# A Mamba-2 step's tokens turned by a transposing DMA instead of by TensorE

## The reference

```python
proj = hidden_states @ in_proj_w.T
gate, hBC, dt = jnp.split(proj, [INTER, INTER + CONV_DIM], axis=-1)
hBC = silu(causal_conv4(hBC) + conv_b)          # channel by channel, along the tokens
hs, Bx, Cx = jnp.split(hBC, [INTER, INTER + G * N], axis=-1)
dt = softplus(dt + dt_bias)
X = hs * dt                                      # tokens of a head, times dt
Y_diag = (C B^T * exp(segsum(A dt))) @ X         # within a chunk
states = (B * decay_to_end) ^T @ X               # of a chunk
Y_off = C @ previous_states * exp(cumsum(A dt))  # between chunks
xg = (Y_diag + Y_off + D * hs) * silu(gate)
out = groupwise_rms_norm(xg) @ out_proj_w.T
```

## Time and profile before

| | |
|---|---|
| median of three runs | 1616.51 us |
| the profiled execution, whole | 1617.07 us |
| its span | 1615.3 us |
| TensorE busy | 1598.4 us (99%) |
| VectorE busy | 1390.4 us (86%) |
| ScalarE busy | 1266.0 us (78%) |
| GpSimd busy | 1168.7 us (72%) |
| DMA queue of the loads | 41.7% of 16 engines |
| granted TensorE clock | 1.0 |

### The profile page before, as it was taken

How to read it: one execution, slowest core, us unless ns; L and a number is a source line. 1 busy time by engine, 2 the same in 40 slices (tenths; PEclk the granted TensorE clock), 3 DMA queues, 4 the chain that set the end, 5 groups by cost and what they waited for, 6 DMA issues and landing times. The chain is left out here.

```text
span 1615.3 us, 29072 instructions
## 1 busy us (share of the span) xinstructions
PE 1598.4 (99%) x9668; PEld 1342.4 (83%) x9668; DVE 1390.4 (86%) x2356; ACT 1266.0 (78%) x2496; POOL 1168.7 (72%) x1496
## 2 busy tenths in 40 slices
PE   8999999999999999999999999999999999999998
PEld 7888888888888888888878888888888888888887
DVE  6988888888888888898889888888888988888887
ACT  3678888888888888878846888888888888888885
POOL 5548777778687776878774587777777768777685
PEclk9999999999999999999999999999999999999999
DMA  5244443444434445344314444444454444434431
GB/s 174 92 150 128 136 143 122 149 129 134 148 118 149 133 130 150 119 146 130 119 51 144 133 131 147 122 145 131 133 150 123 141 134 129 151 126 138 143 120 63
DMA packets 82372, 212.18 MB, mean 131 GB/s; under 512 B 11184, under 2 KB 27568, under 8 KB 81968
## 3 DMA queue, kind: packets, MB, share of 16 engines
q1 hardware_dynamic: 82224, 210.33, 41.7%
HBM read 207.14 MB, written 3.15 MB: 130 GB/s over the span
## 5 line engine op out<-in xcount | busy, mean ns | idle before, releaser
L653 POOL TENSOR_TENSOR xl<-xg,xh 128x256 fp32r<-128x256 f32 x254 | 290.7, 1166 | 319.4 <-ACT xh L482 318.8
L558 POOL TENSOR_TENSOR wl<-raw,wh 128x256 fp32r<-128x256 f32 x584 | 425.4, 758 | 76.6 <-ACT wh L325 76.6
L353 ACT ACTIVATE mt<-cs_row,cs_tok 128x128 f32<-128x128 f32 x1024 | 324.8, 391 | 0.0
L667 POOL TENSOR_TENSOR wol<-raw_o,woh 128x256 fp32r<-128x256 f32 x256 | 181.5, 729 | 30.5 <-ACT woh L472 30.5
L1223 DVE TENSOR_TENSOR mt<-mt,gt 128x1024 f32<-128x1024 f32 x128 | 200.7, 1568 | 0.0
L660 POOL TENSOR_TENSOR sqa<-sqa,sq 128x256 f32<-128x256 f32 x222 | 158.9, 735 | 0.8 <-ACT sq L499 0.8
L482 ACT ACTIVATE xh<-xg 128x512 fp32r<-128x512 f32 x128 | 81.0, 633 | 95.4 <-DVE xg L1203 95.4
L325 ACT ACTIVATE wh<-raw 128x1024 fp32r<-128x1024 f32 (+1 forms) x146 | 152.1, 1042 | 0.8 <-DMA raw<-in_w_dtag 0.8
L1000 DVE SCALAR_TENSOR_TENSOR cv<-bt,par_sb,cv 128x511 f32<-128x511 f32 (+2 forms) x192 | 142.9, 744 | 6.8 <-ACT cv L329 2.3
L1000 DVE SCALAR_TENSOR_TENSOR cv<-bh,par_sb,cv 128x511 f32<-128x511 f32 (+2 forms) x192 | 142.9, 744 | 4.5
L717 PE MATMUL bg<-xTh,wh 128*128 128x512 f32 x544 | 145.8, 390 | 0.0
(11 more groups left out here) (218 smaller groups left out, 3601.7 us busy)
## 6 DMA issues: line engine op xcount, KB each, us to landing
raw<-in_w_step SPq DMA_DIRECT2D x128, 512.0 KB, 3.5
cs_row<-cs_rows SPq DMA_DIRECT2D x128, 512.0 KB, 5.5
raw_o<-in_w_out SPq DMA_DIRECT2D x128, 256.0 KB, 4.1
ec_row<-ec_rows SPq DMA_DIRECT2D x256, 96.0 KB, 4.7
raw<-in_w_bc SPq DMA_DIRECT2D x16, 512.0 KB, 3.6
acc<-in_x SPq DMA_DIRECT2D x8, 256.0 KB, 5.3
cs_row<-in_w_ffn SPq DMA_DIRECT2D x2, 1024.0 KB, 6.6
out_dram<-acc SPq DMA_DIRECT2D x1, 1024.0 KB, 6.2
```

What stands on the lines that cost most here:

```text
L353: e = act.activation(mt[:, m % 2, h, chunk(j)], cs_row[:, m % 2, h, chunk(j)], ACT.Relu, bias=cs_tok[:, j, 2 * m + h:2 * m + h + 1], scale ...
L558: e = pool.tensor_tensor(wl[:, n % 2, cols], raw[:, n % 2, cols], wh[:, n % 2, cols].bitcast(F32), ALU.subtract)
L653: e = pool.tensor_tensor(xl[:, u, cols], xg[:, u, cols], xh[:, u, cols].bitcast(F32), ALU.subtract)
L667: e = pool.tensor_tensor(wol[:, 1 - u, cols], raw_o[:, 1 - u, cols], woh[:, 1 - u, cols].bitcast(F32), ALU.subtract)
```

## The change

The four transposes leave TensorE for all steps of a sequence but the last (126 of 128 steps, m from 0 to 62). In their place:

1. ScalarE copies h2, seen as 1024 numbers of 16 bits per partition, into the buffer `tg` as two planes: all low halves, then all high halves (a_half).
2. SyncE issues one transposing DMA from there into `turned`, 128 partitions by 8 blocks of 128 numbers of 16 bits (ld_turn). It stands ahead of the loads of its iteration.
3. GpSimd joins the halves again with two copies into xt, one for each plane (p_tok).
4. VectorE's `take_tokens` reads xt from SBUF instead of a PSUM bank, and stands behind the three taps instead of ahead of the mask product. Its second product works in place and waits for the first.

The gate's tanh writes `tg` too, so it now waits for the DMA's landing. The small tensors of the router use the memory of `turned` before the steps begin. The last step of each sequence keeps the transposes.

The diff (left out: how the router's small tensors are laid into `spare`):

```diff
--- before.py
+++ after.py
@@ -7,6 +7,7 @@
 
 F32 = mybir.dt.float32
 F32R = mybir.dt.float32r
+U16 = mybir.dt.uint16
 ALU = mybir.AluOpType
 ACT = mybir.ActivationFunctionType
 AXX = mybir.AxisListType.X
@@ -120,6 +121,9 @@
         pick = sb("pick", [P, SQ])
         some = sb("some", [P, L // SQ])
 
+        turned = sb("turned", [P, 2 * NJ, P], U16)
+        halves = tg[:, :].bitcast(U16)
+
         gflat = gt[:, :, :].rearrange("p g c -> p (g c)")
         xn = gflat[:, 0:NJ * HID].rearrange("p (j d) -> p j d", j=NJ)
         um = gflat[:, 6 * L:7 * L].rearrange("p (j c) -> p j c", j=NJ)
@@ -132,18 +136,15 @@
         mv = sb("mv", [P, NJ, 2])
         ve = sb("ve", [P, NJ])
         rstd = sb("rstd", [P, NJ])
+        spare = turned[:, :, :].rearrange("p a b -> p (a b)").bitcast(F32)
...
         dab, dm, de = mt[:, 0, 0], mt[:, 0, 1], mt[:, 1, 0]
         dz, dw, dh, dden = sg[:, 0], sg[:, 1], tg[:, :], mt[:, 1, 1]
@@ -166,6 +167,7 @@
         ld_ec = [sem(f"ld_ec{i}") for i in range(2)]
         st_cs, st_out = sem("st_cs"), sem("st_out")
         v_pick, v_some = sem("v_pick"), sem("v_some")
+        a_half, p_tok, ld_turn = sem("a_half"), sem("p_tok"), [sem(f"ld_turn{i}") for i in range(2)]
         a_dr, p_acc, t_fin, v_xl = sem("a_dr"), sem("p_acc"), sem("t_fin"), sem("v_xl")
 
         pv, pa, pp, pe_ = sem("pro_dve"), sem("pro_act"), sem("pro_pool"), sem("pro_pe")
@@ -198,6 +200,23 @@
 
         def has(m):
             return 0 <= m < STEPS
+
+        def by_dma(m):
+
+            return 0 <= m < STEPS - 1
+
+        def turn(b, m):
+            return b * (STEPS - 1) + m
+
+        def wait_turned(eng, b, m):
+
+            if m < 0:
+                b, m = b - 1, m + STEPS
+            if b >= 0:
+                if by_dma(m):
+                    eng.wait_ge(a_half, did(turn(b, m)))
+                else:
+                    eng.wait_ge(t_t, did(b))
 
         def bank_y(b, m):
 
@@ -295,6 +314,11 @@
                 sp.wait_ge(p_ffn, b + 1)
                 for m in range(-2, STEPS):
                     n = b * STEPS + m
+                    if by_dma(m - 1):
+                        q = turn(b, m - 1)
+                        sp.wait_ge(a_half, did(q))
+                        sp.wait_ge(p_tok, did(q - 1))
+                        sp.dma_start_transpose(turned[:, :, :], halves).then_inc(ld_turn[q % 2], 16)
                     if m + 2 < STEPS or b + 1 < NB:
                         load(step(b, m + 2))
                     if has(m):
@@ -316,7 +340,7 @@
 
         @block.scalar
         def _(act):
-            start(act, (a_dr, a_tap, a_th, a_tg, a_rl, a_ex, a_s1, a_xh, a_sq, a_wh, a_wn, a_woh, a_bt))
+            start(act, (a_half, a_dr, a_tap, a_th, a_tg, a_rl, a_ex, a_s1, a_xh, a_sq, a_wh, a_wn, a_woh, a_bt))
             act.wait_ge(ld_hp, 16)
             act.activation(nA[:, 0:1], hp[:, 1:2], ACT.Exp).then_inc(scaled, 1)
 
@@ -505,6 +529,8 @@
                             tanh_conv(n, u, mine)
                         act.wait_ge(t_g, did(n))
                         act.wait_ge(v_sg, did(n - 1))
+                        if by_dma(m - 1):
+                            act.wait_ge(ld_turn[turn(b, m - 1) % 2], landed(turn(b, m - 1)))
                         act.activation(tg[:, :], bg[:, :], ACT.Tanh, scale=0.5).then_inc(a_tg, 1)
                         if m >= 2:
                             tanh_conv(n, u, mine)
@@ -512,6 +538,12 @@
                         weights_and_state()
                     if m == STEPS and b + 1 < NB:
                         split_ffn(b + 1)
+                    if by_dma(m):
+                        act.wait_ge(v_h2, did(un))
+                        act.wait_ge(v_sg, did(n))
+                        act.activation(halves.rearrange("p (two t) -> p two t", two=2),
+                                       h2[:, u, :].bitcast(U16).rearrange("p (t two) -> p two t", two=2),
+                                       ACT.Copy).then_inc(a_half, 1)
                     if has(m):
                         rises(b, m, 1)
                         act.wait_ge(a_rl, did(n, 2))
@@ -528,7 +560,7 @@
 
         @block.gpsimd
         def _(pool):
-            start(pool, (p_acc, p_wl, p_wol, p_xl, p_sqa, p_rr))
+            start(pool, (p_tok, p_acc, p_wl, p_wol, p_xl, p_sqa, p_rr))
             pool.memset(ident[:, :], 0.0).then_inc(const_ok, 1)
             pool.memset(causal[:, :], 0.25).then_inc(const_ok, 1)
             pool.memset(ones[:, :], 1.0).then_inc(const_ok, 1)
@@ -643,6 +675,14 @@
                             e = pool.tensor_tensor(mt[:, 1 - u, 1, cols], mt[:, 1 - u, 1, cols],
                                                    gt[:, (m - 1) % GROUPS, cols], ALU.mult)
                         e.then_inc(p_m, 1)
+                    if by_dma(m - 1):
+                        q = turn(b, m - 1)
+                        pool.wait_ge(ld_turn[q % 2], landed(q))
+                        pool.wait_ge(t_d, did(n - 2))
+                        to = xt[:, :, :].bitcast(U16).rearrange("p j (c two) -> p two j c", two=2)
+                        for half in range(2):
+                            e = pool.tensor_copy(to[:, half], turned[:, NJ * half:NJ * (half + 1), :])
+                        e.then_inc(p_tok, 1)
                     if m == STEPS - 4 and b + 1 < NB:
                         inverse_dev(b + 1)
                     if m == STEPS + 1 and b + 1 < NB:
@@ -948,7 +988,7 @@
                         sum_parts()
                     if m == STEPS and b + 1 < NB:
                         project_dt(b + 1)
-                    if has(m):
+                    if has(m) and not by_dma(m):
                         pe.wait_ge(v_h2, did(un))
                         for j in range(NJ):
                             mm = pe.transpose(mine[:, chunk(j)], h2[:, u, chunk(j)], ident[:, :])
@@ -1203,17 +1243,24 @@
                         dve.tensor_tensor(xg[:, u, :], yb[:, :], sg[:, u, :], ALU.mult).then_inc(v_xg, 1)
 
                     def take_tokens():
-                        dve.wait_ge(t_t, did(n - 1))
+                        if by_dma(m - 1):
+                            dve.wait_ge(p_tok, did(turn(b, m - 1)))
+                            x_d, x_t = xt[:, 0:NS, :], xt[:, :, :]
+                        else:
+                            dve.wait_ge(t_t, did(b))
+                            x_d = other[:, 0:NS * P].rearrange("p (j c) -> p j c", j=NS)
+                            x_t = other[:, :].rearrange("p (j c) -> p j c", j=NJ)
                         dve.wait_ge(t_st, did(n - 2))
                         if m == 1:
                             dve.wait_ge(pa, b * PRO_ACT + ACT_TABD)
                         dve.tensor_tensor(xd[:, :, :].rearrange("p j (h c) -> p j h c", h=2),
-                                          other[:, 0:NS * P].rearrange("p (j h c) -> p j h c", j=NS, h=2),
+                                          x_d.rearrange("p j (h c) -> p j h c", h=2),
                                           dd_tok[:, :, heads].unsqueeze(3).broadcast_to([P, NS, 2, HD]),
                                           ALU.mult).then_inc(v_xd, 1)
                         dve.wait_ge(t_d, did(n - 2))
+                        dve.wait_ge(v_xd, did(n - 1))
                         dve.tensor_tensor(xt[:, :, :].rearrange("p j (h c) -> p j h c", h=2),
-                                          other[:, :].rearrange("p (j h c) -> p j h c", j=NJ, h=2),
+                                          x_t.rearrange("p j (h c) -> p j h c", h=2),
                                           dt_tok[:, :, heads].unsqueeze(3).broadcast_to([P, NJ, 2, HD]),
                                           ALU.mult).then_inc(v_x, 1)
 
@@ -1233,7 +1280,7 @@
                     if m == STEPS and b + 1 < NB:
                         token_lo(b + 1, 0)
                         token_lo(b + 1, 1)
-                    if has(m - 1) and not ahead:
+                    if has(m - 1) and not ahead and not by_dma(m - 1):
                         take_tokens()
                     if ended is not None:
                         add_group(b, ended)
@@ -1245,6 +1292,8 @@
                     if has(m):
                         for k in range(1, TAPS):
                             tap(n, un, u, mine, k)
+                        if by_dma(m - 1):
+                            take_tokens()
                         if m == 0:
                             dve.wait_ge(t_bt, did(b * GROUPS + GROUPS - 2))
                             mask_scores(b, GROUPS - 2)
@@ -1254,7 +1303,7 @@
                                                      op0=ALU.add, op1=ALU.mult).then_inc(v_sg, 1)
 
                         def conv_product():
-                            dve.wait_ge(t_t, did(n - 2))
+                            wait_turned(dve, b, m - 2)
                             if m == 1:
                                 dve.wait_ge(t_bt, did(b * GROUPS + GROUPS - 1))
                             silu_conv(un, cv[:, u, :], mine, h2[:, u, :])
```

(18 more changed lines are left out.)

## The result

The changed kernel takes 1638.3 us in the median of four runs (1636.1 to 1638.6), where the kernel before took 1616.7 beside it. The ratio is 1.0131, with a 95% interval of 1.0113 to 1.0148: it is slower. 1586 was predicted, and a faster kernel; the range of 1562 to 1665 holds the time.

What follows compares the result with a forecast made beforehand. The prediction took TensorE to set each step, 11.14 us falling to 10.64. Gaining 63 us and losing 32 at group ends leaves 31 off the profiled 1617.07, so 1586 us; the 8-in-10 range was 1562 to 1665.

Steps and rivals of the forecast that it cites:

- TensorE: 0.50 us by 126 steps, 63 us: TensorE's queue: without the four transposes a regular step falls from 11.14 to 10.64 us, 63 us over 126 steps.
- Contention: 0.38 us: VectorE's xd and xt, both inputs now in SBUF beside GpSimd: 0.38 us extra per step, between 0 and 0.76.
- rival 1: Contention at xd and xt costs the full 0.76 us, loop 10.91 in every step, about 1632 us; chance 0.14.
- The first loop: ScalarE from S to cv, VectorE's taps, xd, xt, TensorE's state product: 10.15 us, 10.53 with contention, under 10.64.
- Separation: 0.94 us: ScalarE's copy of 1024 numbers per partition into two planes occupies its queue for 0.94 us; bounds 0.63 and twice 1.04.
- Copies: 1.5 us, reach to 2.8: GpSimd's two copies joining the halves: 0.75 us each, together 1.5; bounds 0.71 and 1.41 each.
- Landing: 4.0 us: Transposing DMA, issue to landing: 4.0 us, between 2.5 and 5.5; its loop of 10.1 us is hidden.
- Rival 2: Landing of 5.5 us makes the DMA's loop 11.6; TensorE waits for xl, about 1690 us; chance 0.28.
- SyncE: nothing: Loads behind the transposing DMA on SyncE, tightest raw_o with 1 to 3 us left: costed at nothing.
- Group ends: 2.1 us over two steps of 10.64: Drains on ScalarE and reductions on VectorE, now barely covered: 2.1 us per group, between 1.2 and 3.0; 15 groups, 32 us.

Runs made afterwards that it cites:

- experiment 1: Changed kernel, copies still made, but xd and xt read whatever lies in a PSUM bank in place of xt: 1600.9 us, ratio 0.9895.
- experiment 3: Kernel before, with the four transposes of each step left out and nothing in their place: 1580.7 us, ratio 0.9774.
- experiment 6: Changed kernel without the transposing DMA; the copies wait for the separation and join zeros: 1647.9 us, ratio 1.0181, steps of 11.21 and 10.75 mixed.
- experiment 5: Changed kernel with ScalarE's wh moved behind cv and sq: 1640.7 us, ratio 1.0142, regular step still 10.94.
- experiment 2: Changed kernel with GpSimd's sqa and wl made for only 8 numbers per piece, both inputs still in SBUF: 1603.2 us, ratio 0.9914.
- experiment 7: Changed kernel with the transposing DMA made twice, the second after the first has landed: 1836.7 us in one run, period 12.56.

## Why the prediction was wrong, step by step

Experiments 1 and 3 split the result into parts by measured medians (the kernel before took 1616.7 to 1618.3 beside them). Without transposes and with nothing in their place 1580.7; with the separation, the DMA, the copies and the new place of the products, but no contention at them, 1600.9; all of it, 1638.3.

**TensorE: 0.50 us by 126 steps, 63 us.** Mis-sized twice. The off-chunk product gives 0.10 back in each step, and the step said that nothing would. And the steps at group ends were not TensorE's: the prediction called them hidden, but at 11.61 they were already beyond 11.14. The ceiling was 37 us.

**Contention: 0.38 us.** This is the step that failed, and rival 1 is what happened. Durations grew by 0.27 for xd and 0.36 for xt, 0.63 together. The prediction took what the mask product pays beside GpSimd, 0.37 us, as a factor of 1.31 on its 1.21, and put the factor on two shorter instructions. The extra does not grow with the length. Here are GpSimd's two pieces of sqa one by one, from the step shown above, in which xd ran from 418.55 to 419.37 and xt from 419.48 to 420.52:

```profile
418.21 0.75 POOL L700 TENSOR_TENSOR sqa<-sqa,sq 128x256 f32<-128x256 f32 x1
...
418.91 1.07 POOL L700 TENSOR_TENSOR sqa<-sqa,sq 128x256 f32<-128x256 f32 x1
```

xd ends 0.42 us behind the first piece, xt 0.55 behind the second, and that second piece, which began during xd, ends 0.60 behind xd. The two engines take turns:

| product | starts | GpSimd's piece ends | product ends | behind the piece | undisturbed |
|---|---|---|---|---|---|
| mask product, before | 420.52 | 421.02 | 422.10 | 1.08 | 1.22 |
| L1085, before | 817.50 | 818.04 | 818.60 | 0.56 | 0.69 as xt |
| xd, changed | 418.55 | 418.96 | 419.37 | 0.42 | 0.55 |
| xt, changed | 419.48 | 419.98 | 420.52 | 0.55 | 0.69 |
| xd, experiment 6, short step | 421.39 | 421.57 | 421.99 | 0.42 | 0.55 |
| xd, experiment 6, long step | 432.14 | 432.80 | 433.22 | 0.41 | 0.55 |

A product takes what is left of the piece that GpSimd is in when it starts, plus its own time less 0.13 us. In the changed kernel this gives, to 0.05 us, the time of all 125 xd and all 111 xt that began with more than 0.16 us of a piece left. So one product can lose anything from nothing to about 0.58 us (an estimate: a piece of 0.71 less 0.13). In the long steps of experiment 6 the two lose 0.89, more than the 0.76 that the prediction had for its upper bound. In experiment 5 xd came 0.12 us behind the start of its piece instead of 0.34, and lost those 0.22 us again.

The first loop was summed to 10.15 us without contention; with 0.63 for it, and 0.11 each for xt's wait for xd and for a state product that now starts late, it is 11.0 less 0.07 at the taps: 10.93, over TensorE's 10.75. Rival 1 was priced at 10.91 per step and 1632 us, by the row of L1085, and was given 0.14. That the range holds 1638 is owed to its upper end, which stood for a slow landing; that landing did not come.

The Trainium skill has a rule for this (SBUF — State Buffer, Who interferes with whom): a VectorE instruction with two inputs in SBUF contends with a GpSimd instruction that reads SBUF, one with a single SBUF input does not (outside VectorE's two-port modes). Experiments 1 and 2 agree on each side. The page also calls the shared ports an exclusive lock, and says for the two-port modes that the loser is blocked for the other's whole instruction; the table agrees with a lock that is held for a whole instruction for these products as well.

**Separation: 0.94 us.** Right: 410.84 to 411.79 is 0.95, and its row reads 1.05.

**Copies: 1.5 us, reach to 2.8.** Right where nothing interferes: 0.78 in the median. Beside VectorE's mask product they are longer (0.96 in the mean of all, 1.85 for the two in the step shown), which stays within the reach.

**Landing: 4.0 us.** Too high, and harmless: part 6 of the page of the profile has 3.1, and the chain was hidden as forecast. Rival 2 was false for this kernel; experiment 7 shows its loop with twice the landing.

```profile
turned<-tg SPq DMA_TRANSPOSE x126, 3.1
```

Plain loads of the same size take 2.5 to 5.3 us, so the Trainium skill's sentence that transposing DMAs are as fast as regular ones (Advanced Engine Details and Errata, X-Bar Transpose) agrees. The 1.7 us on top, an estimate worked out from a figure for earlier generations on the Trainium skill's page DMA: Bandwidth & Descriptors, did not appear.

**SyncE: nothing.** Right. The transposing DMA holds its queue for 1.24 us, and raw_o, issued at 414.36, is used at 419.20.

**Group ends: 2.1 us over two steps of 10.64.** Mis-sized: 23.38 predicted for the pair by this step (23.85 by the sum, which adds 2.1 to a pair that was already 22.75), 24.61 measured. 23.58 of it stands without contention (experiment 1); the rest is again xd and xt.

**Starts of the sequences.** Missing in the prediction. The chain from the separation to the state product was checked against a regular step, where older work covers it, and not against the second step, which has none. It costs 4.2 us twice, and 3.4 without contention (experiment 1), where the sum credited each start with 1.0. About 1.6 us of it is the clock.

Together, by the medians: TensorE gave 37 us and not 63, 26 missed. The longer chain costs 20 us without contention, by the traces 12.5 at the group ends and 7.6 at the starts. Contention at xd and xt costs 37 us, some 19 of it in regular steps and 15 at group ends. Against these 57.6 us stood 31.5 in the forecast; 26.2 + 57.6 - 31.5 is the 52.3 us missed.

Under the next sequence's layer norm five steps take 11.06 to 11.41 us. In the four of 11.2 or more xd takes 0.99 to 1.02 us instead of 0.82, so some 0.18 of their excess of 0.3 or more is contention; the rest is not settled.

## What to carry to other kernels

Before an operand moves from PSUM to SBUF, look at what GpSimd does beside its readers: the operand's place can cost more than the work that it saves. Price it by what is left of GpSimd's running instruction when the reader starts, not by a factor. Count the gain of a relieved engine only in the steps that it sets, and check a longer chain in the first steps too, where nothing covers it and an idle TensorE may also come back at the lower clock. If a loop is set by contention, moving its parts earlier may only move them beside other work, or to another point of the same instruction of GpSimd.

## What was not expected of the hardware

- Contention here is taking turns by whole instructions: the extra of 0.63 us on xd and xt is what was left of two pieces of GpSimd, less 0.13 each, so the mask product of 1024 numbers (0.37) paid what xt of 512 paid (0.36).
- It costs both sides. Beside xd and xt, GpSimd's two pieces of sqa took 1.77 us instead of 1.43 and four of wl 3.24 instead of 2.81: 0.77 us, where VectorE lost 0.63.
- A one-input copy of GpSimd is hit as well: the two copies took 1.85 us beside the mask product and 1.45 without.
- A transposing DMA from SBUF to SBUF, 256 KB in elements of 16 bits, landed 3.1 us after its issue, within the 2.5 to 5.3 of plain loads of that size.
- Removing four transposes that TensorE's timeline showed as 0.50 us shortened the step by 0.39.
- After 4.3 idle microseconds at each sequence's start TensorE ran for 3.4 us at a granted clock of 0.50.
